# Five of eighteen down products per tile as three short-form passes, their squares made twice

## What is computed

```python
x = x + layernorm(attention(layernorm(x)))
h_in = layernorm(x)
combine = top6_of_32_weights(sigmoid(h_in @ gate_w.T))        # zero for experts not chosen
h = square(relu(einsum('th,eih->tei', h_in, up_w))) * combine[:, :, None]
moe = einsum('tei,ehi->th', h, down_w)
shared = square(relu(h_in @ shared_up_w.T)) @ shared_down_w.T
x = x + layernorm(moe + shared)
```

## Time and profile before

| | us |
|---|---|
| median of 3 runs (530.91 to 533.93) | 531.47 |
| the profiled execution's own time | 531.55 |
| its span in the trace | 529.5 |
| feed-forward half in the span, first up product to last down product | 277.5 to 521.8 |
| one of tiles 1 to 5 | 30.37 |

### The profile page before, as it was taken

One profiled execution on the slowest core, in us unless ns is written; L12 is line 12 of the kernel. 1 busy time (PEld: TensorE's weight loads), 2 busy tenths in 40 slices (PEclk: granted clock), 3 DMA queues, 4 the chain that ended last, 5 costly groups with the idle time before them and its releaser, 6 DMA issues.

```text
span 529.5 us, 10851 instructions
## 1 busy us (share of the span) xinstructions
PE 479.3 (91%) x3376; PEld 268.1 (51%) x3376; DVE 400.7 (76%) x1074; ACT 354.9 (67%) x701; POOL 171.8 (32%) x501
## 2 busy tenths in 40 slices
PE   2456999999998999998799999999999999999994
PEld 1222445454444445444346666666656665666662
DVE  4678788899999989888926769596776859585453
ACT  2423788888889988887675566767667666755442
POOL 5045133333535535211002324425153533302021
PEclk9999999999999999999899999999999999999999
DMA  6334444444444344330042244535363544535431
GB/s 177 114 122 127 120 130 132 125 134 131 131 143 137 117 120 122 121 107 32 4 142 68 114 164 157 167 104 200 94 186 108 179 160 138 197 106 176 142 107 40
DMA packets 52744, 67.47 MB, mean 127 GB/s; under 512 B 4560, under 2 KB 36304, under 8 KB 52688
## 3 DMA queue, kind: packets, MB, share of 16 engines
q1 hardware_dynamic: 52688, 66.78, 40.5%
HBM read 51.17 MB, written 15.20 MB: 125 GB/s over the span
## 4 chain that ended last, share of the span: by engine, by line
PE 73%; DVE 9%; ACT 6%; issue 6%; POOL 5%; DMA 0%; POOLq 0%; DVEq 0%; ACTq 0%
PE pS L1316 12%; PE pY L1316 11%; PE pO L1235 8%; PE pS L1179 7%; PE pS L1300 6%; PE pS L1302 6%; PE pS L1301 6%; DVE mneg L865 4%; PE pS L1185 3%; ACT probs L655 3%; PE pX L1164 2%; PE pX L1167 2%; PE pX L1159 1%; PE pY L1262 1%; POOL xn L524 1%
## 5 line engine op out<-in xcount | busy, mean ns | idle before, releaser
L865 DVE TENSOR_REDUCE mneg<-pS 128x2 f32<-128x512 f32 x256 | 164.0, 685 | 23.4 <-PE pS L1179 22.7
L655 ACT ACTIVATE probs<-pS 128x512 f32<-128x512 f32 x256 | 144.2, 595 | 25.6 <-PE pS L1185 23.9
L730 ACT ACTIVATE h_ring<-r 128x512 f32<-128x512 f32 x144 | 90.4, 629 | 88.9 <-DVE r L1034 68.0
L1034 DVE SCALAR_TENSOR_TENSOR r<-pS,c_ring 128x512 f32<-128x512 f32 x128 | 87.6, 689 | 45.6 <-PE pS L1302 44.2
L1179 PE MATMUL pS<-kp,qp 48*128 48x256 bf16 x512 | 87.5, 291 | 18.8 <-DVE mneg L865 10.1
L1300 PE MATMUL pS<-qp,up_hi 128*128 128x512 f32 x144 | 103.5, 719 | 0.0
L1185 PE MATMUL pS<-qp,kp 51*128 51x256 bf16 x512 | 87.6, 282 | 0.9 <-ACT probs L655 0.7
L1235 PE MATMUL pO<-probs,vv 128*32 128x256 f32 x1024 | 74.1, 397 | 0.4 <-ACT oT_sb L606 0.4
L1316 PE MATMUL pS<-h_ring,down_sb 128*128 128x512 f32 x144 | 73.8, 594 | 0.0
L1316 PE MATMUL pY<-h_ring,down_sb 128*128 128x512 f32 x144 | 73.4, 595 | 0.0
L1179 PEld LDWEIGHTS pS<-kp,qp 48*128 48x128 bf16 x512 | 34.1, 96 | 69.0 <-DVE mneg L865 40.5
(11 more groups left out here) (178 smaller groups left out, 679.0 us busy)
## 6 DMA issues: line engine op xcount, KB each, us to landing
c_ring<-c_scratch SPq DMA_DIRECT2D x64, 512.0 KB, 4.0
qp<-q_scratch SPq DMA_DIRECT2D x64, 96.0 KB
kp<-k_scratch SPq DMA_DIRECT2D x64, 96.0 KB
q_scratch<-q_parts SPq DMA_DIRECT2D x16, 192.0 KB, 2.3
k_scratch<-k_parts SPq DMA_DIRECT2D x16, 192.0 KB, 2.4
q_scratch<-q_parts SPq DMA_DIRECT2D x16, 128.0 KB, 2.2
k_scratch<-k_parts SPq DMA_DIRECT2D x16, 128.0 KB, 2.2
out_x<-ot SPq DMA_DIRECT2D x7, 256.0 KB, 4.4
```

The lines of the kernel that those rows point to most:

```text
L655: nc.scalar.activation(probs[j][:, hh], pS2[n % S2_RING][:, :, :], ACT.Exp, scale=SCALE).then_inc(exp_done, 1)
L730: nc.scalar.activation(h_sb[n % HRING], r_sb[n % URING][:, :], ACT.Square).then_inc(sq_done, 1)
L865: nc.vector.tensor_reduce(mneg[u % 2][:, :, hh, k], pS1[n % S1_RING][:, :].rearrange("p (a s) -> p a s", a=TH), AX.X, ALU.max, negate=True ...
L1034: nc.vector.scalar_tensor_tensor(out=r_sb[n % URING][:, :], in0=pU[n % URING], scalar=0.0, in1=c_ring[group % CRING][:, at], op0=ALU.max, ...
```

## The change

In each tile blocks 2, 5, 8, 11 and 14 (SPLIT) get another kind of down product. Line numbers in this section and in its order rows are those of the kernel after where they belong to it.

- **ScalarE** squares such a block twice: first rounded to F32R (h_hi, a ring of three), then whole in f32 into one buffer (h_whole). The second square waits until GpSimd has finished with the block split before (lo_done).
- **GpSimd** subtracts high from whole (low), a 128x512 tensor_tensor, into a ring of two (h_lo). The calls low(i, 0) to low(i, 4) stand between its other work.
- **TensorE** makes the down product of such a block as three F32R passes, high x high, high activation x low weight, low activation x high weight (down_split), six blocks behind the up product (SPLIT_LAG = 6); the other 13 down products stay as they were, three blocks behind.
- **Once per run** GpSimd cuts the five weight blocks into high and low (split_down), after unit 27 of 32 in attention.
- **Room**: the ring of squares has three buffers for the 13 plain blocks; two buffers of c_ring (the broadcast expert weights) and the buffers fn and ot now lie in the attention half's probs, so that the third and fourth load of c_ring wait until the last output product of attention is done (pv_done). root_t shares its memory with comb. keep_fT waits for the tile's last split product.

```diff
-HRING = URING = 4
+HRING, URING = 3, 4
+SPLIT = (2, 5, 8, 11, 14)
+SPLIT_LAG, HI_RING, LO_RING = 6, 3, 2
...
+                if n in (2, 3):
+                    sp.wait_ge(pv_done, 4 * NB)
...
+            def low(i, s):
+                n = FBLK * i + SPLIT[s]
+                at = splits_to(n)
+                pool.wait_ge(hi_done, at + 1)
+                pool.wait_ge(sq_done, n + 1)
+                if at >= LO_RING:
+                    pool.wait_ge(split_done, at - LO_RING + 1)
+                nc.gpsimd.tensor_tensor(h_lo[at % LO_RING], h_whole, h_hi[at % HI_RING].bitcast(F32),
+                                        ALU.subtract).then_inc(lo_done, 1)
...
             for i in range(NTILE):
+                low(i, 0)
                 if i + 2 < NTILE:
                     residual1(i + 2)
+                if i == 0:
+                    low(i, 1)
                 if i + 1 < NTILE:
                     root_of_sum(i + 1)
+                if i >= 1:
+                    low(i, 1)
                 if i + 2 < NTILE:
                     chain_x1(i + 2)
+                low(i, 2)
                 if i >= 1:
                     chain_f(i - 1)
+                low(i, 3)
+                low(i, 4)
                 if i + 3 < NTILE:
                     chain_y(i + 3)
...
+                at = splits_to(n)
+                if n % FBLK in SPLIT:
+                    if at >= HI_RING:
+                        act.wait_ge(split_done, at - HI_RING + 1)
+                    nc.scalar.activation(h_hi[at % HI_RING], r_sb[n % URING][:, :], ACT.Square).then_inc(hi_done, 1)
+                    if at >= 1:
+                        act.wait_ge(lo_done, at)
+                    nc.scalar.activation(h_whole, r_sb[n % URING][:, :], ACT.Square).then_inc(sq_done, 1)
+                    return
...
             def keep_fT(i):
-                act.wait_ge(down_done, FBLK * (i + 1))
+                act.wait_ge(split_done, len(SPLIT) * (i + 1))
...
+                pe.wait_ge(lo_done, at + 1)
+                high, low = h_hi[at % HI_RING], h_lo[at % LO_RING]
+                mm(pF[i % 2], down_hi[:, s], high, start=False, stop=False)
+                mm(pF[i % 2], down_lo[:, s], high, start=False, stop=False)
+                mm(pF[i % 2], down_hi[:, s], low, start=False, stop=s == len(SPLIT) - 1).then_inc(split_done, 1)
...
+                if n >= LAG and (n - LAG) % FBLK not in SPLIT:
+                    down_block(n - LAG)
+                if n >= SPLIT_LAG and (n - SPLIT_LAG) % FBLK in SPLIT:
+                    down_split(n - SPLIT_LAG)
```

More of the change, by code:

```diff
@@ L192, in block_kernel @@
         comb, root, root_c = (sb(n, [P, C4, E]) for n in ("comb", "root", "root_c"))
-        root_v, root_h, root_t = (sb(n, [P, C4, E]) for n in ("root_v", "root_h", "root_t"))
+        root_v, root_h = (sb(n, [P, C4, E]) for n in ("root_v", "root_h"))
+        root_t = comb
         cT = sb("cT", [E, TILE])
-        c_ring = [sb(f"c_ring{i}", [P, CGROUP, TILE]) for i in range(CRING)]
+        c_ring = ([sb(f"c_ring{i}", [P, CGROUP, TILE]) for i in range(2)]
+                  + [probs[i][:, :, :, :].rearrange("p a b c -> p (a b c)").rearrange("p (k t) -> p k t", k=CGROUP)
+                     for i in range(2)])
         r_sb = [sb(f"r{i}", [P, TILE]) for i in range(URING)]
-        h_ring = sb("h_ring", [P, HRING, TILE])
-        h_sb = [h_ring[:, i] for i in range(HRING)]
+        h_ring = sb("h_ring", [P, HRING + 1, TILE])
+        h_whole = h_ring[:, HRING]
+        h_hi, h_lo = ([sb(f"{name}{i}", [P, TILE], F32R)[:, :] for i in range(n)]
+                      for name, n in (("h_hi", HI_RING), ("h_lo", LO_RING)))
+        down_hi, down_lo = (sb(f"down_{n}", [P, len(SPLIT), D], F32R) for n in ("hi", "lo"))
+        down_whole = down_sb[:, :, :].rearrange("p (a b) d -> p a b d", b=3)[:, 0:len(SPLIT), 0]
         fT_sb = sb("fT_sb", [P, TILE])
-        assert HRING * TILE == RBLK * P and TILE >= SI
+        assert all(k - SBLK == 3 * s for s, k in enumerate(SPLIT))
+        assert (HRING + 1) * TILE == RBLK * P and TILE >= SI
         up_in = [h_ring[:, i] for i in range(NCUT - 1)] + [fT_sb[:, 0:SI]]
         w_cut = r_sb[0]
-        fn = sb("fn", [P, C4, D])
-        ot = [sb(f"ot{i}", [P, C4, D]) for i in range(2)]
+        fn = probs[3][:, :, :, :].rearrange("p a b c -> p (a b c)")[:, 0:TILE].rearrange("p (c d) -> p c d", c=C4)
+        ot = [probs[2][:, :, :, :].rearrange("p a b c -> p (a b c)")[:, TILE * i:TILE * (i + 1)]
+              .rearrange("p (c d) -> p c d", c=C4) for i in range(2)]
         pS1 = [ps(f"pS1_{i}", [P, TILE]) for i in range(S1_RING)]
@@ L292, in block_kernel @@
         sq_done = sem("sq_done")
+        hi_done, lo_done = sem("hi_done"), sem("lo_done")
+        split_done = sem("split_done")
+        dhi_done, dlo_done = sem("dhi_done"), sem("dlo_done")
         down_done = sem("down_done")
@@ L312, in x1_bank, with splits_to @@
             return pX[:, :] if i < 2 else pF[(i - 1) % 2]
+        def splits_to(n):
+            i, k = divmod(n, FBLK)
+            return len(SPLIT) * i + sum(at < k for at in SPLIT)
         def part3(eng, wait, b):
@@ L563, in _ @@
                 split_max(u)
+                if u == 27:
+                    split_down()
                 if u == 0:
@@ L1315, in down_block, with down_split, downs @@
                     pe.wait_ge(y_kept, NB)
-                mm(pF[i % 2], down_sb[:, block], h_sb[n % HRING], start=k == 0,
-                   stop=k == FBLK - 1).then_inc(down_done, 1)
+                mm(pF[i % 2], down_sb[:, block], h_ring[:, (n - splits_to(n)) % HRING], start=k == 0,
+                   stop=False).then_inc(down_done, 1)
+            def down_split(n):
+                i, k = divmod(n, FBLK)
+                s, at = SPLIT.index(k), splits_to(n)
+                if n == SPLIT[0]:
+                    pe.wait_ge(dlo_done, 1)
+                pe.wait_ge(lo_done, at + 1)
[3 more added lines that the diff above has]
+                mm(pF[i % 2], down_hi[:, s], low, start=False, stop=s == len(SPLIT) - 1).then_inc(split_done, 1)
+            def downs(n):
+                if n >= LAG and (n - LAG) % FBLK not in SPLIT:
+                    down_block(n - LAG)
+                if n >= SPLIT_LAG and (n - SPLIT_LAG) % FBLK in SPLIT:
+                    down_split(n - SPLIT_LAG)
             def transpose_f(i):
@@ L1464, in _ @@
                             transpose_x1(i + 2)
-            for n in range(FBLK * NTILE - LAG, FBLK * NTILE):
-                down_block(n)
+            for n in range(FBLK * NTILE, FBLK * NTILE + LAG):
+                downs(n)
             transpose_f(NTILE - 1)
```

15 lines of the change are left out of this document (10 added, 5 removed).

## The result

| | before | after |
|---|---|---|
| median, us (6 runs each) | 531.18 (530.34 to 533.93) | 535.81 (535.59 to 536.97) |
| ratio after to before, 95% interval | | 1.0074 (1.0051 to 1.0098) |
| the profiled execution's own time / its span | 531.55 / 529.5 | 536.97 / 535.1 |

The account below looks back on a forecast made before the run. The prediction took TensorE's stream of matmuls to set the time before the change. Its sum: 531.55 + 2.7 (tile 0) + 2.1 (tiles 1 to 5) + 0.1 (tile 6) - 0.1 (tile 7) = 536.3 us, range 527 to 541.5.

Parts of the forecast that it names:

- TensorE's saving: Down products: three passes take 0.70 us in place of 0.86, saving 0.155 each, 0.78 per tile, 6.2 in all.
- The chain round a middle tile: Tiles 1 to 5: exponential to exponential through ScalarE, VectorE and GpSimd takes 30.8 us in place of 30.37, +2.1 in all.
- one rival of 0.13: Shared port: block 2's subtraction holds COPY 1.2 us, line 963 falls under residual1 again; 541.8 us, chance 0.13.
- The prediction's point of decision: Middle tiles: the shared port lengthens the chain once w_sum passes 385.5, later than residual1's end.
- copies of over a microsecond: VectorE: copies lasting this long would show the forecast wrong and the shared port right.
- Only tile 0 pays: Middle chain 1.2 us shorter than added up, so TensorE paces tiles 1 to 7: 529.6 us, chance 0.22.
- only the matmuls count: GpSimd and ScalarE keep up everywhere, so all of TensorE's 6.2 us is saved: 525.4 us, chance 0.15.
- Tile 0: First tile: TensorE and ScalarE wait for block 8's subtraction, ready at 305.1: +2.7 us, work saved included.
- Tile 6: Open chain: exponential 0.7 us later, TensorE waits some 0.9 for block 6's square, less 0.78 saved: +0.1 us.
- Tile 7: Last tile: saves 0.78 us and pays 0.70 for the product alone at the end: -0.1 us.
- Costed at nothing: split_down in attention lies in GpSimd's idle time; uncovered it would cost 3 us once. Also c_ring loads, rings, keep_fT.

Follow-up runs that it names:

- passes and squares: The kernel after with second squares but without GpSimd's subtractions, the third pass taking the high part again: 526.96 us.
- distance 4: The kernel before with all down products four blocks behind in place of three: 530.67 us, ratio 0.9985.
- two buffers: The kernel after with two buffers for the whole square in place of one: 530.79 us, ratio 0.997.
- passes alone: The kernel after without second squares and without GpSimd's subtractions, the third pass taking the high part again: 529.39 us.
- the best: The kernel after with two whole-square buffers, plain down products four blocks behind, split ones seven, and larger rings: 526.79 us, ratio 0.9902.
- unread subtractions: The kernel after with GpSimd subtracting buffers of its own that nobody waits for, the third pass taking the high part again: 530.45 us.
- both edits of tile 0: The kernel after with two whole-square buffers and, in tile 0, block 8's subtraction before root_of_sum and chain_x1: 532.31 us, ratio 1.0013.

## Why the prediction was right, and where it was not

**TensorE's saving: right, a little small.** Each pass of a split product is 0.23 us after the one before. With three of them a block step takes 389.88 - 388.50 = 1.38 us, where a full product's took 1.55, so a product saves 0.17, not 0.155:

```profile
388.50 0.39 PE L1359 MATMUL pS<-qp,up_lo 128*128 128x512 f32 x1
388.73 0.40 PE L1383 MATMUL pY<-h_hi,down_hi 128*128 128x512 f32 x1
...
389.88 0.39 PE L1359 MATMUL pS<-qp,up_lo 128*128 128x512 f32 x1
```

TensorE by itself needs 29.35 us for a middle tile (passes and squares), not 29.6. The difference is these 5 x 0.015 and a wait of some 0.18 us per tile that the kernel before had already (30.36 against 30.18 with distance 4), and that I had counted as TensorE's work.

**The chain round a middle tile: right, in each of its three parts.** From the exponential's end to residual1's start 388.93 - 378.37 = 10.56 (10.4 + 0.1 said); from there to the end of block 11's subtraction 402.01 - 388.93 = 13.08 (12.9); from there to the next exponential's end 409.13 - 402.01 = 7.12 (7.4). Together 30.76, 30.8 said. That this chain is what paces the tile, and that the single h_whole closes it, the two buffers showed: 0.7 us per tile less, from one buffer. The prediction had only this one cost in a middle tile. There are two of about the same size: take the chain away and 0.7 us go (30.77 to 30.07), take the held COPY away as well and another 0.7 go (30.07 to 29.35). In after the second lies hidden behind the first; that the chain alone, without the held COPY, would give the same 30.8, no run shows.

**The held COPY: a rival, and no harm to the number.** I gave VectorE's holds one rival of 0.13, with COPY and line 963 held together. Half of it came true: COPY was held, line 963 was not. In after this changes nothing, because the 1.1 us lost at one place were gained at the other, and w_sum was ready at 390.14 + 0.24 = 390.38, with root_of_sum at 390.46. The prediction's point of decision (w_sum 11.9 us behind the exponential's end; measured 390.38 - 378.37 = 12.0) was just reached: residual1 ended at 390.35, so root_of_sum hardly lost anything. The forecast owed something to luck here. The prediction had also named copies of over a microsecond as a sign that it was wrong; the sign came (1.27 us) and the time stood all the same, so it was the wrong sign: w_sum against residual1's end was the one to watch.

**The second rival's figure was wrong.** "Only tile 0 pays" would have been 529.6 by TensorE's pace. With the chain open the time is 530.79, because the hold then paces the tile at 30.07. I had taken TensorE to be what is left once the chain is open; it was a third limit, VectorE's first half of the tile with the hold in it, and it is worth 0.7 us of each middle tile. The same holds for "only the matmuls count" (525.4): passes alone gave 529.39, with residual1 holding line 963's successor; where nothing was held it was 526.96.

**Tile 0: right.** Block 8's subtraction starts at 305.14, less the 1.47 by which all is later 303.67 (303.8 said); the last up pass of step 15 is at 307.74, or 306.27 (306.3 said). From the trace of after, ScalarE and TensorE waiting for that subtraction:

```profile
306.44 0.63 ACT L783 ACTIVATE h_ring<-r 128x512 f32<-128x512 f32 x1 [3.31 <-POOL h_lo L596]
306.46 0.50 PE L1383 MATMUL pS<-h_hi,down_hi 128*128 128x512 f32 x1 [1.43 <-POOL h_lo L596]
```

The tile came out at +2.31 for +2.7.

**Tile 6: the number right, the reason wrong.** -0.07 for +0.1. The wait for block 6's square is there, as predicted, but not because the exponential comes later: it comes 3.35 us behind block 0's third up pass in after, 3.10 before, and 3.29 in passes alone, where tile 6 takes 28.92 without that wait. The held COPY makes it: with the chain open by two buffers and the COPY held, tile 6 takes 29.62 as in after (29.67). So it is the same 0.7 us as in the middle tiles, and the +0.1 was right by luck.

**Tile 7: right.** -0.67 + 0.54 = -0.13 for -0.1: what tile 7 saves, the product alone at the end takes back.

**Costed at nothing.** split_down cost nothing that shows in every execution, but nothing is not proven. With it in the kernel the third pass of the first up product comes at 278.11 to 281.18 in the profiled executions (278.39 with two buffers, 278.14 in the best), against 278.10 and 277.99 in the two without it. Of the +1.47 in after's execution 0.65 us were there before split_down began (at 228.23). Most of the rest came at 234.77, where TensorE waits 1.60 us for a DMA that copies mT (0.42 at that place before). Such a delay at that place shows in four of the ten executions with split_down and in neither of the two without it; whether split_down has a part in it stays open. After's profiled execution is also the slowest of its six, 1.2 us above the median, so this hardly touches the medians.

## What to carry to other kernels

When work is moved off the engine that bounds a kernel, add up the chain that leads round the loop through all engines, with the new operations in each queue; busy shares of 70% and 42% said nothing here. A single buffer between two engines can close such a chain: one more buffer gave back 5 us, one more step of distance (with the buffers that it needs) 4 more. And look at what else runs at the moments when a long GpSimd operation does: moving residual1 by one microsecond changed a middle tile by 0.7 us, because it no longer held one of VectorE's operations.

## What the runs showed of the hardware

- **A small COPY is held too.** A float32 COPY of 128x16 on VectorE takes 0.17 us, and 1.27 when a subtraction of 128x512 runs on GpSimd; it ends when that ends (384.72 and 384.70 in after's tile 3). The prediction had this for operations with two inputs in SBUF, which the runs confirm at two more places (0.28 to 1.38 and 0.29 to 1.34). The Trainium skill (GPSIMD Engine Reference, section 8, Key points) names instructions in a two-port mode beside those with two SBUF inputs. The COPY has one input, so by that page it would be of the first kind; its 1.27 agrees, but no row tells an instruction's mode. Rectifications with one input in PSUM kept their 0.69 us on average in after (its two groups at line 1091: 686 and 688 ns).
- **The hold is as long as GpSimd's operation.** 0.73 us of subtraction over 256 columns held the COPY for 0.72. It seems to go the other way too: residual1 takes 1.42 us where it starts 0.03 us behind VectorE's line 1020 of 0.28 us (388.93 and 388.90 in after), and 1.30 where that operation lies before it. The Trainium skill (SBUF — State Buffer, section SBUF: two separate sides) calls the shared pair an exclusive lock for the whole instruction of whoever starts first. The COPY's numbers agree; residual1's agrees in direction only, since it is 0.12 us longer where 0.25 us of line 1020 were left to run.
- **Writing F32R costs GpSimd nothing:** the 40 subtractions of 128x512 take 1287 ns on average in after, where they write F32R, and 1288 in the kernel with unread subtractions, where they write f32.
- **The clock can fall behind a wait of 2.1 us in the second half,** to 0.50 for 3.4 us in one execution (both edits of tile 0), and stay at 1.00 behind the same wait in another.
